# Moving the inverse square roots of two transformer layers from VectorE to GpSimd

## The reference, cut to what matters

```
x = _layernorm(x + _L0_attn_ref(x, ...))      # q, k divided by their norm over all 128 columns; softmax over 1024 keys; 16 heads of 8
x = _layernorm(x + _L0_ffn_ref(x, ...))       # int8 quantized 128 -> 128 product
x = _layernorm(x + _L1_attn_ref(x, ...))      # layer norm of each head's 8 values of q and k, rotary embedding, causal softmax
x = _layernorm(x + _L1_ffn_ref(x, ...))       # silu(gate) * up, 128 -> 384 -> 128
...
def _layernorm(x, axis=-1, eps=1e-05):
    m = jnp.mean(x, axis=axis, keepdims=True)
    v = jnp.var(x, axis=axis, keepdims=True)
    return (x - m) / jnp.sqrt(v + eps)
```

## Time and profile before

| | us |
|---|---|
| median of 3 runs | 812.29 (812.27 to 813.13) |
| profiled execution, whole | 812.69 |
| profiled execution, span of its instructions | 810.6 |
| ScalarE busy | 767.8 (95%) |
| TensorE busy | 791.2 (98%) |
| VectorE busy | 528.8 (65%) |
| GpSimd busy | 174.3 (22%) |

### The profile page before, as it was taken

One profiled execution on the slowest core, in us unless ns is written; L12 is line 12 of the kernel. 1 busy time (PEld: TensorE's weight loads), 2 busy tenths in 40 slices (PEclk: granted clock), 3 DMA queues, 4 the chain that ended last, 5 costly groups with the idle time before them and its releaser, 6 DMA issues.

```text
span 810.6 us, 18434 instructions
## 1 busy us (share of the span) xinstructions
PE 791.2 (98%) x7467; PEld 295.0 (36%) x7469; DVE 528.8 (65%) x1422; ACT 767.8 (95%) x869; POOL 174.3 (22%) x370
## 2 busy tenths in 40 slices
PE   8999999999999999999999999999999999999996
PEld 4333333333333433433333333343333343444444
DVE  4353747858758788587863685766563387786656
ACT  4999999999999999999999999999999999999982
POOL 3111101101102601033100521023300263363220
PEclk9999999999999999999999999999999999999999
DMA  5776322415414711442250431231231241053010
GB/s 148 256 230 216 122 79 81 155 41 181 144 35 156 266 40 44 179 156 80 92 208 27 128 106 43 91 128 44 91 131 51 68 131 54 27 190 110 2 28 15
DMA packets 48554, 88.71 MB, mean 109 GB/s; under 512 B 5201, under 2 KB 14545, under 8 KB 48465
## 3 DMA queue, kind: packets, MB, share of 16 engines
q1 hardware_dynamic: 47696, 85.95, 31.2%
q0 software_dynamic: 288, 1.05, 0.4%
q10 hardware_dynamic: 480, 0.48, 0.2%
HBM read 50.50 MB, written 35.65 MB: 106 GB/s over the span
## 4 chain that ended last, share of the span: by engine, by line
PE 73%; ACT 13%; DVE 9%; issue 4%; POOL 1%; DMA 0%; ACTq 0%; DVEq 0%; POOLq 0%
PE ps L896 35%; PE ps L874 20%; ACT probs L717 13%; PE ps L763 8%; PE ps L752 3%; PE ps L849 2%; DVE th L1282 1%; DVE hT L1283 1%; PE ps L930 1%; PE ps L757 1%; DVE sums_t L1137 0%; POOL v_all L590 0%; PE ps L938 0%; PE ps L791 0%; DVE gate_sb L1279 0%
## 5 line engine op out<-in xcount | busy, mean ns | idle before, releaser
L717 ACT ACTIVATE probs<-ps 128x1024 f32<-128x1024 f32 x800 | 745.8, 1057 | 17.6 <-PE ps L874 13.8
L896 PE MATMUL ps<-probs,v_st 128*32 128x512 f32 (+3 forms) x3584 | 424.9, 556 | 3.1 <-issue 1.8
L874 PE MATMUL ps<-q_st,k_st 32*128 32x512 f32 (+3 forms) x1792 | 257.0, 458 | 3.2 <-ACT probs L717 2.3
L874 PEld LDWEIGHTS ps<-q_st,k_st 32*128 32x128 f32 x1792 | 119.4, 181 | 289.5 <-ACT probs L717 240.7
L627 POOL TENSOR_SCALAR_AFFINE_SELECT probs<-probs 128x256 f32<-128x256 f32 x256 | 103.8, 428 | 139.1 <-ACT probs L717 137.0
L896 PEld LDWEIGHTS ps<-probs,v_st 128*32 128x32 f32 x3584 | 80.1, 108 | 109.2 <-issue 80.3
L595 POOL COPY v_st<-v_all 128x256 f32<-128x256 f32 (+1 forms) x65 | 25.7, 405 | 342.1 <-PE ps L896 334.2
L1256 DVE COPY mid_qkv<-ps 128x384 f32<-128x384 f32 x32 | 17.8, 557 | 44.3 <-PE ps L763 43.8
L1137 DVE STREAM_TRANSPOSE sums_t<-ps 128x512 f32<-128x512 f32 x32 | 22.9, 717 | 26.6 <-PE ps L896 26.5
L1287 DVE TENSOR_TENSOR last_y<-ps,last_y 128x128 f32<-128x128 f32 x24 | 7.0, 292 | 42.7 <-PE ps L763 42.7
L849 PE MATMUL ps<-yTp,w_hid 128*128 128x512 f32 x84 | 30.8, 448 | 2.2 <-DVE hT L1283 0.6
(11 more groups left out here) (192 smaller groups left out, 645.2 us busy)
## 6 DMA issues: line engine op xcount, KB each, us to landing
k_st<-parts_scratch SPq DMA_DIRECT2D x46, 512.0 KB, 3.6
parts_scratch<-mid_part SPq DMA_DIRECT2D x34, 512.0 KB, 3.8
q_st<-parts_scratch SPq DMA_DIRECT2D x62, 256.0 KB, 3.9
parts_scratch<-prep_part SPq DMA_DIRECT2D x28, 512.0 KB, 4.0
k_st<-parts_scratch SPq DMA_DIRECT2D x17, 256.0 KB, 2.8
xT<-in_xT SPq DMA_DIRECT2D x8, 256.0 KB, 4.4
x_all<-in_x SPq DMA_DIRECT2D x8, 256.0 KB, 6.5
out<-yo SPq DMA_DIRECT2D x7, 256.0 KB, 2.3
```

The costliest lines, as they stand in the source:

```text
L717: nc.scalar.activation(probs[:, k % PS, :, 0:w], slot(k)[:, :, 0:w], ACT.Exp).then_inc(probs_ready, 1)
L874: last_ = mm(slot(k)[:, e, at:at + n], k_st[row, p % KB, kt * P:(kt + 1) * P], q_st[row, p % KB, lo:HALF], start=True, stop=not shifted)
L896: last_ = mm(acc[HR * h:HR * (h + 1), lo:HALF], v_st[:, p % VB, kt, h, :], probs[:, (2 * s + h // 2) % PS, h % 2, at:at + n], start=FIRST[ ...
```

## The change

All units `ln_rs1`, `ln_rs2`, `rs1`, `rs2` of the table become GpSimd's. [...] Two new groups of semaphores join them: `stats_made` (VectorE's `ln_aggr` or `norms` to GpSimd) and `root_made` (GpSimd to `ln_out` or `scale`). In GpSimd's list the roots stand in their slot with priority 4, behind the masks of the step before. The roots of the first two chunks and of the tail stay on VectorE. `ORDER` is replaced by another table with the same 202 TensorE units, 256 instead of 344 VectorE units and 88 GpSimd units.

```diff
-LN_UNITS = [("dve", n, 0) for n in ("ln_stats", "ln_aggr", "ln_rs1", "ln_rs2", "ln_out")]
+LN_UNITS = [("pool" if n in ("ln_rs1", "ln_rs2") else "dve", n, 0) for n in ("ln_stats", "ln_aggr", "ln_rs1", "ln_rs2", "ln_out")]
+ROW_UNITS = [("pool" if n in ("rs1", "rs2") else "dve", n, 0) for n in ("square", "norms", "rs1", "rs2", "scale")]
...
 ORDER = """
...
+        root_chain = Chain(pool, sem("pool_own"))
+        def roots(name, c, what, k):
+            if what in ("ln_rs1", "ln_rs2"):
+                own_, n, s_ = lane(name, c), root_number(name, c, k), tok[lane(name, c)]["st"]
+                x, y, t = s_[:, 1, 0:TC], s_[:, 2, 0:TC], s_[:, 3, 0:TC]
+                if what == "ln_rs1":
+                    pool.wait_ge(stats_made[own_], n)
+                    root_chain.link(g_.tensor_scalar(x, s_[:, 0, :].rearrange("p (t a) -> p t a", a=2)[:, :, 1], LN_EPS, None, ALU.add))
...
+            link, mul = root_chain.link, lambda out, a_, b_: g_.tensor_tensor(out, a_, b_, ALU.mult)
+            if what in ("ln_rs1", "rs1"):
+                link(g_.tensor_scalar(y.bitcast(I32), x.bitcast(I32), -0.5, float(RSQRT_SEED), ALU.mult, ALU.add))
+                link(mul(t, y, y))
+                link(mul(t, t, x))
+                link(g_.tensor_scalar(t, t, -RSQRT_STEP, RSQRT_STEP * 2.38924456, ALU.mult, ALU.add))
+                link(mul(y, t, y))
+            else:
+                z = s_[:, 1, 0:TC] if what == "ln_rs2" else x
+                link(mul(t, y, y))
+                link(mul(t, t, x))
+                link(g_.tensor_scalar(z, t, 0.375, -1.25, ALU.mult, ALU.add))
+                link(mul(t, z, t))
+                link(g_.tensor_scalar(t, t, 1.875, None, ALU.add))
+                mul(y, t, y).then_inc(root_made[own_], 1)
...
+        todo += [(s, 4, "root", (name, c, what, k)) for s in range(NS + 1) for name, c, e, what, k in SIDE_ORDER[s] if e == "pool"]
         todo.sort(key=lambda x: x[:2])
...
             else:
+                dve.wait_ge(root_made[name], number)
                 for t in range(TC):
                     op = ts(dst[:, t, :], src[:, t, :], s_[:, 0, 2 * t:2 * t + 1], s_[:, 2, t:t + 1], ALU.subtract, ALU.mult)
...
             elif what == "scale":
+                dve.wait_ge(root_made[name + "_rows"], root_number(name, c, None))
                 op = tt(by(out[:] if name == "prep" else qk), by(qk), bc(per(1).unsqueeze(3), wide), ALU.mult)
```

More of the change, by code:

```diff
@@ L105, in first_slot @@
     return (2 * FIRST[p] - 3) // 2 if p else 0
[L109 removed]
+LN_UNITS = [("pool" if n in ("ln_rs1", "ln_rs2") else "dve", n, 0) for n in ("ln_stats", "ln_aggr", "ln_rs1", "ln_rs2", "ln_out")]
+ROW_UNITS = [("pool" if n in ("rs1", "rs2") else "dve", n, 0) for n in ("square", "norms", "rs1", "rs2", "scale")]
 QKT = [("pe", "qkT", 1), ("pe", "qkT", 0)]
 PREP = [("pe", "qkv", t) for t in range(TC)] + \
[L112 removed]
+       ROW_UNITS + QKT
 MID = LN_UNITS + \
@@ L117 @@
       [("pe", "normT", 0)] + [("pe", "qkv", t) for t in range(TC)] + \
-      [("dve", n, 0) for n in ("square", "norms", "rs1", "rs2", "scale", "rope0", "rope1", "rope2", "rope3")] + QKT
+      ROW_UNITS + [("dve", n, 0) for n in ("rope0", "rope1", "rope2", "rope3")] + QKT
 LAST = LN_UNITS + [("pe", "normT", 0)] + \
@@ L129, in lane, with root_number @@
     return "mid" if (name, c) == ("last", NCH - 2) else name
+def root_number(name, c, k):
+    if k is None:
+        return c - 1 if name == "prep" else c + 1
+    return 2 * (NCH if (name, c) == ("last", NCH - 2) else c) + k + 1
 def norm_number(name, c):
@@ L157 @@
 ORDER = """
[L158 to L174, removed]
@@ L394, in program @@
     own = {n: sem(f"{n}_own") for n in ("prep", "mid", "last", "turn")}
+    stats_made = {n: sem(f"{n}_stats") for n in ("mid", "last", "prep_rows", "mid_rows")}
+    root_made = {n: sem(f"{n}_root") for n in stats_made}
     xq_ready = sem("xq_ready")
@@ L666, in _ @@
                 mask(n)
+            elif what == "root":
+                roots(*n)
             elif what == "load":
@@ L1055, in _, with layernorm @@
         side_t = side.rearrange("p (t c) -> p t c", t=TC)
-        def layernorm(name, what, src, dst, done=None):
+        def layernorm(name, what, src, dst, done=None, number=0):
             ch, s_, bn = chain[name], tok[name]["st"], tok[name]["bn"]
@@ L1064, in layernorm @@
                 for t in range(TC):
-                    ch.step(v.bn_aggr(s_[:, 0, 2 * t:2 * t + 2], bn[:, t, :]))
+                    op = v.bn_aggr(s_[:, 0, 2 * t:2 * t + 2], bn[:, t, :])
+                    op.then_inc(stats_made[name], 1) if number and t == TC - 1 else ch.step(op)
+                if number:
+                    return
                 ch.need()
@@ L1099, in rows_norm @@
             elif what == "norms":
-                ch.link(v.tensor_reduce(per(0), by(sq[:]), AX.X, ALU.add))
+                v.tensor_reduce(per(0), by(sq[:]), AX.X, ALU.add).then_inc(stats_made[name + "_rows"], 1)
             elif what == "rs1":
[L1102 to L1105, removed]
+                ch.link(ts(s_[:, 0, 0:n], s_[:, 0, 0:n], 1e-24, None, ALU.max))
                 rsqrt_first(v, ch, s_[:, 1, 0:n], s_[:, 0, 0:n], s_[:, 2, 0:n])
@@ L1157, in piece @@
                 if what == "ln_out":
-                    layernorm(ln, what, x_all[:, c], y1, norm_ready[ln] if name == "last" else None)
+                    layernorm(ln, what, x_all[:, c], y1, norm_ready[ln] if name == "last" else None, root_number(name, c, k))
                 elif what == "ln_out_x":
-                    layernorm(ln, what, y2, x_all[:, c], norm_ready[ln])
+                    layernorm(ln, what, y2, x_all[:, c], norm_ready[ln], root_number(name, c, k))
                 elif what == "ln_out_y":
@@ L1317, in units @@
             for name, c, e, what, k in items:
-                read(name, c, what, k) if e == "pe" else piece(name, c, what, k)
+                if e != "pool":
+                    read(name, c, what, k) if e == "pe" else piece(name, c, what, k)
         first_consts()
```

41 lines of the change are left out of this document (34 added, 7 removed).

## The result

The changed kernel takes 826.6 us (824.95 to 827.09), the kernel before 812.3: 14.3 us more by the medians, 1.7% by the ratio, 1.0166 (1.0153 to 1.0180). The forecast was 811.2 with a range up to 816.5, so direction and range are both wrong. The profiled execution has a span of 823.1 us against 810.6; it was the fastest of the four, at a mean granted clock of 0.999, and the three others, 1.2 to 2.1 us longer, had 0.993 to 0.996.

What follows compares the result with a forecast made beforehand. ScalarE and TensorE, both nearly full and taking turns, bound the kernel. Relief -1.5, masks +0.2 and last units +0.2 sum to -1.1: 811.6 profiled, 811.2 us median; own range 809.8 to 812.9, 8-in-10 range 808.3 to 816.5.

Steps and rivals of the forecast that it cites:

- VectorE's relief, -1.5: VectorE loses 86 us of roots; only ScalarE's gaps near 307, 360, 387 and 389 us go, saving 1.5 us.
- The price of a root, 2.9 us: On GpSimd a small root takes 12 links of 0.24 us, 2.9 us, against 1.8 on VectorE.
- the sum allowed 4.3 us a root: At chunk 7's second layer norm, a small root may take 2.9 + 1.4 us before ScalarE notices.
- The step that failed: the waits: VectorE's wait for roots costs 0; masks late behind roots at slots 371, 372 and 135 to 137 cost 0.2 us.
- the three signs of being wrong: GpSimd small product 0.35 us or more; `ln_out` waiting over 1.4 us with new ScalarE gaps; `sums` mask waits beyond 2 us.
- The end of the steps, 0.2: Last table units: chunk 6's second norm, split over slots 397 to 400, finishes just in time before `turn`; 0.2 us booked.
- The table, 0: Rest of the new table: 32 of 40 tens of slots hold the same TensorE units, so 0, bounds -3 and +2.
- The shared path to SBUF, 0: GpSimd roots meeting long VectorE products could lose up to 1.2 us each; most run during PSUM copies, so 0.
- roots too long: GpSimd chains over 4.3 us delay `ln_out` before `normT` and `scale` before rope, `m` lane: 816.6 us, chance 0.21.

Runs made afterwards that it cites:

- short roots on VectorE: Kernel before, old table, roots on VectorE cut from 9 to 3 linked instructions (both polynomial steps left out): 811.0 us, ratio 0.9979.
- slot 191 read first: Kernel before, one table word changed: VectorE reads the q/k/v product before the second half of chunk 7's q/k root: 812.5 us, ratio 0.9999.
- the one with three links: Changed kernel with 3 instead of 12 linked instructions per root on GpSimd (both polynomial steps left out): 815.3 us, ratio 1.0034.
- the swapped word: Changed kernel, slot 77 only: second half of chunk 1's layer norm root put before chunk 4's q/k norm and root: 823.1 us, ratio 1.0130.
- the four roots moved back: Changed kernel with slot 77's order swapped and four of its 44 roots, layer norms of chunks 3, 5, 7, 5, back on VectorE: 819.6 us, ratio 1.0084.

## Why the prediction was wrong, point by point

Three runs lead from the kernel before to the changed one, with one change at each step, by their medians: before 812.3; short roots on VectorE 811.0; the same on GpSimd 813.4; with the new table 815.3; at full length 826.6. So -1.3 for the relief, +2.4 for the move, +1.9 for the table and +11.3 for the length. The forecast had -1.5, 0, 0 and +0.4. The steps depend on their order (with full roots on VectorE the new table alone costs 12 us), but each is a measured difference.

1. *VectorE's relief, -1.5.* Right in size: -1.7 with short roots in the old kernel. The places are only half right, so the size owes something to luck: with short roots the trace gains 0.2 us behind 307 us, 0.4 behind 360 and 0.3 behind 387, 0.8 of the 1.5 booked there, and another 1.0 in small pieces later. Of the 0.42 and 0.46 us only the first was the root's (short roots, slot 191 read first, and layer 0's roots on GpSimd all leave the second).

2. *The price of a root, 2.9 us.* Off by one seventh (3.3), mostly through the link of 0.08 instead of 0.05 us. That 0.05 came from one pair; another linked pair in the same stretch of the kernel before had 0.23 (0.81 + 0.20, the next at 1.24). The 305 us of GpSimd against 320 forecast are no better hit: busy time leaves the pauses between links out, and the forecast had them in. With them the roots hold the queue for 36 x 3.3 + 8 x 5.8 = 165 us, forecast 146. This alone would have passed, for the sum allowed 4.3 us a root.

3. *The step that failed: the waits.* "At 2.9 I book 0", with a limit of 4.3 us, and "I book 0.2 together (bounds 0 and 1.6)" for the masks. A root alone takes 3.3 us, under that limit, and 11.3 us were lost by length all the same. I had priced one root, by itself behind two masks, at one place, the second norm of chunk 7. There the estimate held: `ln_out` waited 3.47 us, and from slot 342 to 348 the changed kernel loses nothing against the one with three links.

```profile
684.62 1.11 DVE L1128 TENSOR_SCALAR x_all<-mid_y,mid_tok 128x128 f32<-128x128 f32 x4 [3.47 <-POOL mid_tok L650]
```

Elsewhere in the queue of GpSimd a root is not alone: at slot 81 half of another root made 5.1 us of it, and a bias add slowed `ln_out` behind it (2.07 us lost), and in the mask stretches half a root of 1.6 us falls on an engine that has no rest for 14 us (0.8 at slot 234, 1.1 at 373, about 1.0 at 195). I had put masks at "up to 1.5 us" per slot; the timeline shows bursts of 2.2 to 2.4 us of them, with a v copy and a bias add of 1.3 us between. The two runs on just such places, the swapped word and the four roots moved back, gave 7.0 us together by the medians, 5.6 in the traces. Against three links the changed kernel's trace loses 9.6 us: 6.5 at slots 81, 195, 234, 241, 341 and 373, the rest in pieces of 0.4 us or less. Two of the three signs of being wrong came: `ln_out` waited 4.1 us at slot 81 with a new gap of 1.8 us behind it, and `sums` waited 5.9 us on masks; the small product, at 0.20 us, was not the fault. The sum also had no term for a lower clock: a standstill of TensorE was followed by one in several of the runs. In the changed kernel's profiled execution that did not happen before the last exponential; with the old table and full roots on GpSimd it was 41 us.

4. *The end of the steps, 0.2.* About right: `ln_out_y` ends and `turn` starts at 801.6, the last `sums` end at 801.34.

```profile
798.47 2.87 PE L945 MATMUL ps<-probs,v_st 128*32 128x512 f32 x24
```
```profile
800.56 1.11 DVE L1128 TENSOR_SCALAR yo<-mid_y,mid_tok 128x128 f32<-128x128 f32 x4 [4.68 <-POOL mid_tok L650]
801.59 0.71 DVE L1188 STREAM_TRANSPOSE sums_t<-ps 128x512 f32<-128x512 f32 x1
```

5. *The table, 0.* Wrong by 1.9 us: with short roots on GpSimd the new table takes 815.3, the old one 813.4. Counting units per ten slots hid that three slots hold two units of TensorE, which share one PSUM bank. The gaps stand right behind them, and splitting the slots takes those gaps away but makes a v copy late; whether another split would return the time was not tried, so why the new table is slower with short roots stays open.

6. *The shared path to SBUF, 0.* Right for the chains: their tensor_tensor has a median of 199 ns and a minimum of 192, so few links met a long VectorE product. It counted where the roots shift a bias add beside VectorE: for `ln_out` at slot 81 (2.03 us instead of 1.12), and for the add at slot 113 of the run with only layer 0's roots on GpSimd (1.70 instead of 0.69).
The Trainium skill's "SBUF — State Buffer", section "Who interferes with whom", lets a VectorE instruction in a two-port mode and a GpSimd instruction block each other for a whole length; the 2.03 us of `ln_out` against 1.12 fits that, without proving which mode it ran in.

The rival "roots too long" had direction and place (`ln_out` ahead of `normT`), but its condition, more than 4.3 us for a small chain by itself, did not hold, its 816.6 is still 10 us short, and it got 0.21. No version that was run and computes the whole reference beats the kernel before.

## What to carry to other kernels

An engine with 22% of its time in use is not free: look at the stretches in which its work is due. Before moving a chain there, lay its length between the instructions that already stand in that queue at each place, and count who waits for those. Count what stands behind the chain's own wait too, for an engine that takes its work in order holds that back even when the chain is short (1.5 us at slot 234 with three links). With a table as tight as this one the loss grows faster than the length, and where TensorE comes to stand, look at its clock behind the standstill before you put all of the loss down to the wait. Here fewer links cost less on either table, but no version with fewer links that still computes the whole root was tried.

## What the runs showed that I had not expected

On GpSimd the next linked instruction starts 0.08 us behind the end of a 0.20 us one: 0.28 us a link, where VectorE's small roots mostly go on at 0.20. And 49 us can be lost to 88 queue entries of 1.6 to 3 us on an engine that is then 36% busy; 21 of them without any engine waiting for the entries themselves. The loss feeds itself: standstills of TensorE of 1.5 to 2.7 us went with its lower clock ten times in that execution, and in one of these stretches a matmul of `sums` took 847 ns instead of 498.
